# Routed tiles of a mixture-of-experts kernel: x transposed by DMA in 16-bit halves instead of by TensorE

## The chip, the cores and the metric

One Trainium2 chip; the kernel runs on one core of it. The metric is the device time of one execution in microseconds (us), lower is better. The engines are TensorE (PE in the profile; its weight loads are PEld), VectorE (DVE), ScalarE (ACT), GpSimd (POOL) and SyncE (SP), which only issues DMAs here.

## The reference

All numbers are float32. Two blocks run one after the other on 2048 tokens of width 256.

```python
x = x + xattn(layernorm(x), k, bias, ctx, ctx, 8)     # 256-tap causal convolutions of head products
x = x + ffn(layernorm(x))
# ffn, for all tokens xt (2048, 256):
scores = softmax(xt @ Wg.T)                           # 16 experts in 4 groups
# the best 2 groups by their maximum, in them the best 4 experts; weights = scores of these
h = silu(einsum('td,eid->eti', xt, W1)) * einsum('td,eid->eti', xt, W3)   # inner width 176
y = einsum('etd,te->td', einsum('eti,edi->etd', h, W2), combine)
z = silu(xt @ Ws1.T) * (xt @ Ws3.T) @ Ws2.T           # shared expert, inner width 352
return y + z
```

## The kernel before

The tokens are 16 units of 128. **First stage** (about 0 to 133 us): for each unit, ScalarE normalises, TensorE convolves with Toeplitz matrices (L1271, L1273), VectorE multiplies, and `norm2(u)` (L502) writes the unit's second layernorm into the first 256 columns of `rows[:, u, :]`. TensorE transposes these (`transpose_xn`) for the router and for the shared expert. A row of `rows` is 288 float32: 256 of x, then 16 gate weights and 16 destination numbers (together the "gates"). VectorE works the routing out in four batches of units; its exponentials are on ScalarE (L516). GpSimd scatters each row with four indirect DMAs (L661) to its four experts' regions of a DRAM buffer, `rows_scratch`.

**Second stage** (about 133 to 198 us): the shared expert (L1424, L1437), while VectorE ends the routing and writes the list of tiles.

**Third stage** (about 198 us to the end): 72 routed tiles of 128 rows of one expert, each engine with its own order of the steps. Tiles 16 to 23 are mixed: 64 rows of each of two experts. Of tile t:
- SP, `gather`: one plain DMA of 128 whole rows (144 KB) from `rows_scratch` into `xg[b]`, four buffers deep (L368); tiles 64 to 71 go to places in `rows` and are issued early (L410). Before each, SP loads the tile's start row from memory into a register and waits until tile t-4 has been transposed by TensorE and its gates taken by VectorE. Between the gathers SP issues other experts' weights, reads of results (L392) and stores.
- TensorE, in each step t: `up(t)` (L1382), `turn_x(t+1)` (L1403: two 128x128 transposes of the gathered rows into PSUM), `down(t-2)` (L1456), `turn_h(t-1)` (L1392).
- ScalarE, in each step: `silu(t)` (L553), `src_tr(t+1)` (L547: copies the transposed x from PSUM to `x_tr`), `store_y(t-2)` (L559).
- VectorE, in each step: `take(t)` (L1126: picks the expert's gate and destination), `hidden(t)` (L1089), `copy_h(t-1)` (L1096), `place(t)` (L1131: writes the destinations for the scatter, after the scatter of tile t-4 has landed). In steps 3 to 6 of each 8 from tile 32 on, one of four adds (L1200 to L1208) of results read back follows.
- GpSimd scatters each tile's y to `y_scratch` (L716).

Of the kernel before, what the change touches and what calls it, by code (L numbers as in the profile page):

```python
# [22 lines left out]
ACT = mybir.ActivationFunctionType  # L23
# [3 lines left out]
I32 = mybir.dt.int32  # L27
U32 = mybir.dt.uint32

P = 128  # L30
# [40 lines left out]
def build(nc, x_d, ctx_d, ctxt_d, ctxr_d, toep_d, bias_d, wg_d, experts_d, ws13_d, ws2_d, out_d):  # L71
    rows_d = nc.dram_tensor("rows_scratch", ((E + 1) * REGION, ROW), F32, kind="Internal").ap()
    y_d = nc.dram_tensor("y_scratch", (TOPK * TOK + 2 * E * P, L), F32, kind="Internal").ap()

    with ExitStack() as ctx:
# [26 lines left out]
        resid = sb("resid", [P, UNITS, L])  # L102
        rows = sb("rows", [P, UNITS, ROW])
# [6 lines left out]
        ident = sb("ident", [P, P])  # L110
        sum_i = sb("sum_i", [P, 2, 32])
        blocks = sb("blocks", [P, P])
# [37 lines left out]
        def carve(n):  # L150
# [47 lines left out]
        xt_ps = [bank[i][:, 0:L].rearrange("p (b n) -> p b n", b=LB) for i in (6, 7)]  # L198
# [15 lines left out]
        row_ready, xt_done, xnt_all = sem("row_ready"), sem("xt_done"), sem("xnt_all")  # L214
# [7 lines left out]
        rows_in = [sem(f"rows_in{b}") for b in range(DEPTH)]  # L222
        xtr_ps, xtr_ready, up_done, silu_done, hid_ready, ht_done, htr_ready, dn_done = (
            sem("xtr_ps"), sem("xtr_ready"), sem("up_done"), sem("silu_done"), sem("hid_ready"), sem("ht_done"),
# [8 lines left out]
        others_in = [sem(f"others_in{b}") for b in range(DEPTH)]  # L233
# [3 lines left out]
        block = ctx.enter_context(nc.Block())  # L237

# [36 lines left out]

        def rows_landed(eng, t, b, before):

            if is_late(t):
                eng.wait_ge(late_in[t - LIVE + LATE], 16)
            else:  # L280
                eng.wait_ge(rows_in[b], before * 16 + 16)

# [8 lines left out]
        def _(sp):  # L291
# [62 lines left out]

            def gather(t, b, before):
                if not (isinstance(t, int) and t < DEPTH):
                    sp.wait_ge(xtr_ps, t - (DEPTH - 1))
                    sp.wait_ge(taken, t - (DEPTH - 1))
                at = sp.value_load(tile_row[0:1, bass.ds(t, 1)], min_val=0, max_val=E * REGION)
# [3 lines left out]
                if is_mixed(t):  # L363
                    sp.dma_start(xg[b][0:HALF], rows_d[bass.ds(at, HALF)]).then_inc(rows_in[b], 16)
                    also = sp.value_load(other_row[0:1, t - MIXED0:t - MIXED0 + 1], min_val=0, max_val=E * REGION + HALF)
                    sp.dma_start(xg[b][HALF:P], rows_d[bass.ds(also, HALF)]).then_inc(others_in[b], 16)
                else:
                    sp.dma_start(xg[b], rows_d[bass.ds(at, P)]).then_inc(rows_in[b], 16)  # L368
# [96 lines left out]
        def _(act):  # L465
# [58 lines left out]
            for u in range(UNITS):  # L524
# [1039 lines left out]
```

## Time and profile before

| what | value |
|---|---|
| time, median of 3 runs | 398.21 us (396.35 to 399.11) |
| profiled execution, first to last instruction | 395.4 us (the profile gives no other time for it) |
| TensorE busy | 384.7 us, 97% |
| VectorE busy | 244.1 us, 62% |
| ScalarE busy | 162.9 us, 41% |
| GpSimd busy | 180.3 us, 46% |
| mean granted TensorE clock | 0.998 |

The page gives busy times of each engine, then groups of instructions by line with their count, busy time, mean and idle time before them. The trace behind it gives the same by stretch and in order of time.

### The profile page before, as it was taken

Reading aid. Unit: us, or ns where it says so; the run is one execution under the profiler, and the core shown is the slowest. Engines: PE = TensorE matmul, PEld = TensorE weight load, DVE = VectorE, ACT = ScalarE, POOL = GpSimd, SP = SyncE. Lnnn points to the kernel's source line nnn. Section 1 sums busy time; section 2 is a strip of 40 time slices with the busy share of each in tenths; the row PEclk is TensorE's granted clock in tenths of the full one; section 3 lists DMA queues with packets and bytes.
Section 4 is the critical chain, followed back from the end, with each engine's and each line's share of the span. In section 5 each row is a group of like instructions: output and inputs, shape, how many; then the busy total and the mean of one; then the engine's idle time right before and its main releaser. Section 6 shows DMA issues by size and latency. Waiting matters only on the chain.

```text
span 395.4 us, 9070 instructions
## 1 busy us (share of the span) xinstructions
PE 384.7 (97%) x2146; PEld 279.3 (71%) x2147; DVE 244.1 (62%) x676; ACT 162.9 (41%) x494; POOL 180.3 (46%) x225
## 2 busy tenths in 40 slices
PE   6999999999999999999999999999999999999996
PEld 6788888888888546555667675446767777777765
DVE  3577577987988465788735344443445464646466
ACT  5347656564564362101124333333333333334431
POOL 3254323337888573565553333333333333334333
PEclk9999999999999999999999999999999999999999
DMA  7974474368879996256376873334474737362737
GB/s 248 363 254 139 163 277 144 133 206 278 309 250 335 414 419 258 96 207 223 104 215 219 321 239 107 87 95 134 127 246 136 242 115 242 115 232 103 264 97 251
DMA packets 37812, 83.09 MB, mean 210 GB/s; under 512 B 5930, under 2 KB 25870, under 8 KB 35728
## 3 DMA queue, kind: packets, MB, share of 16 engines
q1 hardware_dynamic: 31248, 64.83, 49.1%
q0 software_dynamic: 6528, 17.84, 11.6%
q8 instruction: 16, 0.26, 0.3%
q14 instruction: 20, 0.16, 0.1%
HBM read 60.21 MB, written 23.48 MB: 212 GB/s over the span
## 4 chain that ended last, share of the span: by engine, by line
PE 79%; DVE 10%; DMA 4%; issue 2%; ACT 2%; SPq 1%; DVEq 1%; POOL 0%; POOLq 0%
PE heads L1382 18%; PE bank L1456 13%; PE heads L1271 11%; PE heads L1424 7%; PE heads L1273 5%; PE bank L1437 5%; PE heads L1392 4%; PE bank L1403 4%; PE bank L1285 3%; DVE kv L734 3%; PE heads L1374 3%; DMA toep<-toep_in 2%; PE bank L1448 2%; DVE prod L763 2%; DMA y_scratch<-toep,dest_i 2%
## 5 line engine op out<-in xcount | busy, mean ns | idle before, releaser
L716 POOL DMA_INDIRECT y_scratch<-toep,dest_i x72 | 71.8, 997 | 112.0 <-DVE dest_i L1131 96.0
L1382 PE MATMUL heads<-experts,toep 128*128 x256 | 86.6, 461 | 0.6 <-DVE toep L1089 0.5
L1271 PE MATMUL heads<-toep,kv 128*128 128x256 f32 x256 | 77.9, 386 | 1.9 <-DVE kv L734 0.8
L661 POOL DMA_INDIRECT rows_scratch<-rows,slot_i x64 | 63.3, 989 | 35.4 <-issue 19.5
L1456 PE MATMUL bank<-experts,toep 88*128 x256 | 66.2, 381 | 1.6 <-DVE toep L1096 1.6
L553 ACT ACTIVATE toep<-heads 128x176 f32<-128x176 f32 x72 | 22.8, 317 | 78.1 <-PE heads L1382 67.2
L1382 PEld LDWEIGHTS heads<-experts,toep 128*128 128x128 f32 x256 | 43.7, 190 | 14.8 <-issue 1.1
L1273 PEld LDWEIGHTS heads<-toep,kv 128*128 128x128 f32 x256 | 48.7, 190 | 6.5
L763 DVE TENSOR_TENSOR prod<-heads,ctx_rep 128x1024 f32<-128x1024 f32 x32 | 39.1, 1221 | 22.3 <-PE bank L1285 19.9
L1096 DVE COPY toep<-heads 88x256 f32<-88x256 f32 x72 | 30.2, 419 | 31.1 <-PE heads L1392 31.1
L1273 PE MATMUL heads<-toep,kv 128*128 128x128 f32 x256 | 49.2, 274 | 0.0
L1456 PEld LDWEIGHTS bank<-experts,toep 88*128 88x128 f32 x256 | 43.7, 190 | 6.1 <-issue 2.3
L559 ACT ACTIVATE toep<-bank 128x256 f32<-128x256 f32 x72 | 27.6, 383 | 39.5 <-PE bank L1456 34.1
L1424 PE MATMUL heads<-xn_tr_all,ws 128*128 128x512 f32 (+1 forms) x96 | 43.5, 596 | 0.0
L1089 DVE SCALAR_TENSOR_TENSOR toep<-toep,heads 128x176 f32<-128x176 f32 x72 | 28.6, 398 | 23.2 <-ACT toep L553 18.1
L1271 PEld LDWEIGHTS heads<-toep,kv 128*128 128x128 f32 x256 | 38.8, 192 | 2.6 <-issue 1.4
L734 DVE TENSOR_TENSOR kv<-bank,ctx_tr 128x2048 f32<-128x2048 f32 x15 | 34.2, 2282 | 0.1
L1403 PEld LDWEIGHTS bank<-ident,toep 128*128 128x128 f32 x128 | 17.3, 141 | 18.8 <-issue 12.4
L1424 PEld LDWEIGHTS heads<-xn_tr_all,ws 128*128 128x128 f32 (+1 forms) x96 | 16.9, 181 | 19.0 <-issue 18.4
L547 ACT ACTIVATE toep<-bank 128x256 f32<-128x256 f32 x72 | 27.5, 382 | 5.7 <-PE bank L1403 5.5
L1392 PE MATMUL heads<-ident,toep 128*88 128x128 f32 x144 | 27.8, 275 | 0.0
L1126 DVE COPY toep<-toep 128x2 f32 x56 | 10.1, 180 | 24.1 <-issue 15.1
(240 smaller groups left out, 513.4 us busy)
## 6 DMA issues: line engine op xcount, KB each, us to landing
ctx_rep<-ctxr_in SPq DMA_DIRECT2D x16, 1024.0 KB, 5.0
experts<-experts_in SPq DMA_DIRECT2D x16, 608.0 KB
toep<-rows_scratch SPq DMA_DIRECT2D x56, 144.0 KB
prod<-y_scratch SPq DMA_DIRECT2D x5, 1024.0 KB, 5.5
rows_scratch<-pad_row SPq DMA_DIRECT2D x17, 144.0 KB, 1.8
ctx_tr<-ctxt_in SPq DMA_DIRECT2D x16, 128.0 KB
toep<-toep_in SPq DMA_DIRECT2D x4, 512.0 KB, 7.0
ctx_n<-ctx_in SPq DMA_DIRECT2D x16, 128.0 KB, 2.1
```

What stands on the lines that cost most here:

```text
L661: pool.indirect_dma_start(rows_d, bass.IndirectOffsetOnAxis(ap=slot_i[:, u, k:k + 1].bitcast(U32), axis=0), rows[:, u, :], None).then_inc( ...
L716: pool.indirect_dma_start(y_d, bass.IndirectOffsetOnAxis(ap=dest_i[b][:, 0:1].bitcast(U32), axis=0), y_sb[b], None, bounds_check=TOPK * TO ...
L734: nc.vector.tensor_tensor(kv[:, u % 2, :, :].rearrange("p b (g i j) -> p (b g) i j", i=C, j=C), tr_ps.rearrange("p b (g i) -> p (b g) i", ...
L763: nc.vector.tensor_tensor(prod[:, par, :, :], y_ps[par], ctx_rep[:, u % 2, par::2, :], ALU.mult).then_inc(prod_ready, 1)
L1096: nc.vector.tensor_copy(hid_tr[p], ht_ps[p]).then_inc(htr_ready, 1)
L1271: nc.tensor.matmul(y_ps[par][:, i, :], kv[:, q, 0, h * P:(h + 1) * P], toep[:, q * HH + h, :], start=True, stop=False)
L1273: last = nc.tensor.matmul(y_ps[par][:, i, P:], kv[:, q, 1, h * P:(h + 1) * P], toep[:, q * HH + h, 0:P], start=False, stop=True)
L1382: last = nc.tensor.matmul(up_ps[p], x_tr[p][:, blk, :], up_w(e, blk), start=blk == 0, stop=blk == LB - 1)
L1392: last = nc.tensor.transpose(ht_ps[p][:, c, :], hid[p][:, c * HI:(c + 1) * HI], ident[:])
L1403: last = nc.tensor.transpose(xt_ps[p][:, blk, :], src[:, blk * P:(blk + 1) * P], ident[:])
L1424: last = nc.tensor.matmul(bank[2 * (s % 2) + w][0:rows_c, :].rearrange("p (u n) -> p u n", u=GT), ws13[:, blk, w, c0:c0 + rows_c], xn_tr_a ...
L1456: last = nc.tensor.matmul(dn_ps[p], hid_tr[p][:, c, :], down_w(e, c), start=c == 0, stop=c == 1)
```

## The change

x of a routed tile no longer passes TensorE and PSUM. ScalarE writes the layernorm of a unit into one buffer `xn` (TensorE transposes from there), and a new step `split_row` copies it, seen as 16-bit words, into `rows` with all low halves first and then all high halves. The scatter moves the same bytes, declared 16-bit. SP's gather becomes a DMA transpose of the 512 halves of 128 rows: it lands as four blocks of 128x128 halves, already transposed. VectorE puts low and high halves side by side again in `x_tr` (`weave`), for tile t+2 in step t, after `copy_h` and before `place`. `turn_x` and `src_tr` go. The gates come by a DMA of their own (128 bytes of each row) that ScalarE issues after `silu(w-2)` once the tile's x has landed; `take` waits for it. ScalarE's `store_y` of a tile stays at the same place of its order beside TensorE's. SP and ScalarE load four tiles' start rows at once into four registers.

```diff
+    halves_d = rows_d.bitcast(U16)
...
+        xn = sb("xn", [P, L])
...
+        def xn_of(u):
+            return spread[:] if u == UNITS - 1 else xn[:]
...
+        def in_halves(mem):
+            return mem[:, 0:L].bitcast(U16)
...
+            if is_mixed(t):
+                eng.wait_ge(others_in[b], (t - MIXED0) // DEPTH * 16 + 16)
+        def gates_landed(eng, t, b, before):
+            eng.wait_ge(gates_in[b], before * 16 + 16)
+            if is_mixed(t):
+                eng.wait_ge(other_gates[b], (t - MIXED0) // DEPTH * 16 + 16)
...
+            def turned(mem, at, lo, count):
+                return sp.dma_start_transpose(in_halves(mem).rearrange("p (r n) -> p r n", n=P)[:, :, lo:lo + count],
+                                              halves_d[bass.ds(at, count), 0:2 * L])
+            row_of, also_of, late_of = ([sp.alloc_register(f"{n}_of{b}") for b in range(DEPTH)] for n in ("row", "also", "late"))
             def gather(t, b, before):
+                if b == 0:
+                    sp.load(row_of, tile_row[0:1, bass.ds(t, DEPTH)])
+                    if is_mixed(t):
+                        sp.load(also_of, other_row[0:1, t - MIXED0:t - MIXED0 + DEPTH])
+                at = sp.snap(row_of[b], min_val=0, max_val=E * REGION)
                 if not (isinstance(t, int) and t < DEPTH):
-                    sp.wait_ge(xtr_ps, t - (DEPTH - 1))
-                    sp.wait_ge(taken, t - (DEPTH - 1))
-                at = sp.value_load(tile_row[0:1, bass.ds(t, 1)], min_val=0, max_val=E * REGION)
+                    sp.wait_ge(xtr_ready, t - (DEPTH - 1))
                 if isinstance(t, int) and t in (0, DEPTH):
                     need = sp.value_load(tile_need[0:1, t // DEPTH:t // DEPTH + 1], min_val=16 * TOPK * PACED, max_val=16 * TOPK * UNITS)
                     sp.wait_ge(scattered, need)
                 if is_mixed(t):
-                    sp.dma_start(xg[b][0:HALF], rows_d[bass.ds(at, HALF)]).then_inc(rows_in[b], 16)
-                    also = sp.value_load(other_row[0:1, t - MIXED0:t - MIXED0 + 1], min_val=0, max_val=E * REGION + HALF)
-                    sp.dma_start(xg[b][HALF:P], rows_d[bass.ds(also, HALF)]).then_inc(others_in[b], 16)
+                    turned(xg[b], at, 0, HALF).then_inc(rows_in[b], 16)
+                    also = sp.snap(also_of[b], min_val=0, max_val=E * REGION + HALF)
+                    turned(xg[b], also, HALF, HALF).then_inc(others_in[b], 16)
                 else:
-                    sp.dma_start(xg[b], rows_d[bass.ds(at, P)]).then_inc(rows_in[b], 16)
+                    turned(xg[b], at, 0, P).then_inc(rows_in[b], 16)
...
-                at = sp.value_load(tile_row[0:1, t:t + 1], min_val=0, max_val=E * REGION)
-                sp.dma_start(rows[:, UNITS - LATE + j, :], rows_d[bass.ds(at, P)]).then_inc(late_in[j], 16)
+                if j % DEPTH == 0:
+                    sp.load(late_of, tile_row[0:1, t:t + DEPTH])
+                at = sp.snap(late_of[j % DEPTH], min_val=0, max_val=E * REGION)
+                turned(rows[:, UNITS - LATE + j, :], at, 0, P).then_inc(late_in[j], 16)
...
                 act.wait_ge(b2, u + 1)
-                nc.scalar.activation(rows[:, u, 0:L], resid[:, u, :], ACT.Identity,
-                                     bias=ln2[:, u, 4:5], scale=ln2[:, u, 3:4]).then_inc(row_ready, 1)
+                if 1 <= u < UNITS - 1:
+                    act.wait_ge(xt_done, u)
+                nc.scalar.activation(xn_of(u), resid[:, u, :], ACT.Identity,
+                                     bias=ln2[:, u, 4:5], scale=ln2[:, u, 3:4]).then_inc(xn_ready, 1)
+            def split_row(u):
+                act.wait_ge(xn_ready, u + 1)
+                nc.scalar.activation(in_halves(rows[:, u, :]).rearrange("p (s l) -> p s l", s=2),
+                                     xn_of(u).bitcast(U16).rearrange("p (l s) -> p s l", s=2), ACT.Copy
+                                     ).then_inc(row_ready, 1)
...
+                if u >= 2:
+                    split_row(u - 2)
...
-            def src_tr(w, p):
-                if not (isinstance(w, int) and w < 2):
-                    act.wait_ge(up_done, w - 1)
-                act.wait_ge(xtr_ps, w + 1)
-                nc.scalar.activation(x_tr[p], xt_ps[p], ACT.Copy).then_inc(xtr_ready, 1)
+            gate_row, gate_also = ([act.alloc_register(f"{n}_of{b}") for b in range(DEPTH)] for n in ("gate_row", "gate_also"))
+            def load_gates(w, b, before):
+                rows_landed(act, w, b, before)
+                if b == 0:
+                    act.load(gate_row, tile_row[0:1, bass.ds(w, DEPTH)])
+                    if is_mixed(w):
+                        act.load(gate_also, other_row[0:1, w - MIXED0:w - MIXED0 + DEPTH])
+                at = act.snap(gate_row[b], min_val=0, max_val=E * REGION)
+                if not (isinstance(w, int) and w < DEPTH):
+                    act.wait_ge(taken, w - (DEPTH - 1))
+                gates = rows_of(w, b)[:, L:]
+                if is_mixed(w):
+                    act.dma_start(gates[0:HALF], rows_d[bass.ds(at, HALF), L:]).then_inc(gates_in[b], 16)
+                    also = act.snap(gate_also[b], min_val=0, max_val=E * REGION + HALF)
+                    act.dma_start(gates[HALF:P], rows_d[bass.ds(also, HALF), L:]).then_inc(other_gates[b], 16)
+                else:
+                    act.dma_start(gates, rows_d[bass.ds(at, P), L:]).then_inc(gates_in[b], 16)
...
             copy_xn(UNITS - 1)
+            split_row(UNITS - 2)
             silu_shared(2)
+            split_row(UNITS - 1)
             copy_logits(UNITS - 1)
...
-            def routed_step(t, b, before):
+            def routed_step(w, b, before):
                 p = b % 2
-                silu(t, p)
-                if not (isinstance(t, int) and t == LIVE - 1):
-                    src_tr(t + 1, 1 - p)
-                if not (isinstance(t, int) and t < 2):
-                    store_y(t - 2, p, (b - 2) % DEPTH, before if b >= 2 else before - 1)
-            routed(act, routed_step, 2 * DEPTH)
-            for t in range(LIVE - 2, LIVE):
+                if not (isinstance(w, int) and w < 2):
+                    silu(w - 2, p)
+                load_gates(w, b, before)
+                if not (isinstance(w, int) and w < 4):
+                    store_y(w - 4, p, b, before - 1)
+            routed(act, routed_step, MIXED0 + MIXED + DEPTH)
+            for t in range(LIVE - 4, LIVE):
+                if t < LIVE - 2:
+                    silu(t + 2, t % 2)
...
-                        rows_d, bass.IndirectOffsetOnAxis(ap=slot_i[:, u, k:k + 1].bitcast(U32), axis=0),
-                        rows[:, u, :], None).then_inc(scattered, 16)
+                        halves_d, bass.IndirectOffsetOnAxis(ap=slot_i[:, u, k:k + 1].bitcast(U32), axis=0),
+                        rows[:, u, :].bitcast(U16), None).then_inc(scattered, 16)
...
+            def weave(w, b, before):
+                if not (isinstance(w, int) and w < 2):
+                    dve.wait_ge(up_done, w - 1)
+                rows_landed(dve, w, b, before)
+                nc.vector.tensor_copy(x_tr[b % 2].rearrange("p b n -> p (b n)").bitcast(U16).rearrange("p (n s) -> p n s", s=2),
+                                      in_halves(rows_of(w, b)).rearrange("p (s n) -> p n s", s=2)).then_inc(xtr_ready, 1)
...
-                rows_landed(dve, t, b, before)
+                gates_landed(dve, t, b, before)
...
+                if not (isinstance(t, int) and t >= LIVE - 2):
+                    weave(t + 2, (b + 2) % DEPTH, before + 1 if b >= 2 else before)
...
+            for w in range(2):
+                weave(w, w, 0)
             for m in range(4):
                 steps(m, 0, 8)
-            with dve.Fori(4, 8) as m:
+            with dve.Fori(4, 7) as m:
                 steps(m, 0, 8, m - 4, m * 2 - 8)
+            steps(7, 0, 8, 3, 6)
...
-                pe.wait_ge(row_ready, u + 1)
+                pe.wait_ge(xn_ready, u + 1)
                 if u >= 1:
                     pe.wait_ge(xnt_all, u)
                     pe.wait_ge(logits_ready, u)
                 for blk in range(LB):
-                    last = nc.tensor.transpose(xn_ps[:, blk, :], rows[:, u, blk * P:(blk + 1) * P], ident[:])
+                    last = nc.tensor.transpose(xn_ps[:, blk, :], xn_of(u)[:, blk * P:(blk + 1) * P], ident[:])
...
-            def turn_x(t, p, b, before):
-                src = rows_of(t, b)
-                rows_landed(pe, t, b, before)
-                if is_mixed(t):
-                    pe.wait_ge(others_in[b], (t - MIXED0) // DEPTH * 16 + 16)
-                if not (isinstance(t, int) and t < 2):
-                    pe.wait_ge(xtr_ready, t - 1)
-                for blk in range(LB):
-                    last = nc.tensor.transpose(xt_ps[p][:, blk, :], src[:, blk * P:(blk + 1) * P], ident[:])
-                last.then_inc(xtr_ps, 1)
...
-            turn_x(0, 0, 0, 0)
...
                 up(t, p, b)
-                if not (isinstance(t, int) and t == LIVE - 1):
-                    turn_x(t + 1, 1 - p, (b + 1) % DEPTH, before + 1 if b == DEPTH - 1 else before)
```

## Rows read from the trace of the kernel before

**Rows 1.** The page, busy time and share of the span by engine.
```profile
PE 384.7 (97%) x2146; PEld 279.3 (71%) x2147; DVE 244.1 (62%) x676; ACT 162.9 (41%) x494; POOL 180.3 (46%) x225
```
**Rows 2.** Windows: start:end, span, busy by engine (instructions), PE clock, DMA share, GB/s.
```profile
305.00:325.00 20.00, 20.00 (x98) 14.82 (x97) 10.82 (x36) 7.86 (x24) 7.95 (x9) 1.00 0.54 177
```
**Rows 3.** TensorE in order of time, one tile: start, duration, line, tiles, count.
```profile
300.27 1.35 PE L1382 MATMUL heads<-experts,toep 128*128 x4
301.45 0.38 PE L1403 MATMUL bank<-ident,toep 128*128 128x128 f32 x2
301.67 1.03 PE L1456 MATMUL bank<-experts,toep 88*128 x4
302.54 0.39 PE L1392 MATMUL heads<-ident,toep 128*88 128x128 f32 x2
302.76 1.35 PE L1382 MATMUL heads<-experts,toep 128*128 x4
```
**Rows 4.** TensorE's lines L1403 and L1382 alone: durations min/median/max ns, first and last start.
```profile
L1403 PE MATMUL bank<-ident,toep x128: 271/273/329, 197.1 to 361.3; 128*128 128x128 f32 x128
L1403 PE MATMUL bank<-ident,rows x16: 272/273/273, 363.7 to 381.2; 128*128 128x128 f32 x16
...
L1382 PE MATMUL heads<-experts,toep x256: 457/460/558, 198.6 to 383.3; 128*128 x128
```
**Rows 5.** VectorE in order of time; in brackets the idle time before and its releaser.
```profile
293.70 0.15 DVE L1131 CAST dest_i<-toep 128x1 int32<-128x1 f32 x1 [0.78 <-DMA y_scratch<-toep,dest_i]
294.59 0.17 DVE L1126 COPY toep<-toep 128x2 f32 x1 [0.74 <-DVE dest_i L1131]
294.90 0.40 DVE L1089 SCALAR_TENSOR_TENSOR toep<-toep,heads 128x176 f32<-128x176 f32 x1
295.21 0.41 DVE L1096 COPY toep<-heads 88x256 f32<-88x256 f32 x1
295.55 0.14 DVE L1131 CAST dest_i<-toep 128x1 int32<-128x1 f32 x1
295.61 0.68 DVE L1200 TENSOR_TENSOR prod<-prod 128x512 f32<-128x512 f32 x1
296.29 0.17 DVE L1126 COPY toep<-toep 128x2 f32 x1
...
302.96 0.42 DVE L1096 COPY toep<-heads 88x256 f32<-88x256 f32 x1 [0.56 <-PE heads L1392]
```
**Rows 6.** Waits from 230 to 390 us: total us, times, longest.
```profile
DVE dest_i L1131 <- DMA y_scratch<-toep,dest_i: 2.4, 5, 0.8
```
**Rows 7.** Groups by line, ScalarE: busy us, mean ns, idle before.
```profile
L502 ACT ACTIVATE rows<-resid,ln 128x256 f32<-128x256 f32 x16 | 9.6, 600 | 0.5
```
**Rows 8.** DMA view: the queue of SP, and issues with KB each and us to landing.
```profile
q1 hardware_dynamic: 31248, 64.83, 49.1%
...
toep<-rows_scratch SPq DMA_DIRECT2D x56, 144.0 KB
...
y_scratch<-toep,dest_i POOLq DMA_INDIRECT x72, 2.9
...
rows<-rows_scratch SPq DMA_DIRECT2D x8, 144.0 KB, 2.5
```
**Rows 9.** SP's queue in order of time.
```profile
292.46 0.33 SPq L410 DMA_DIRECT2D rows<-rows_scratch  x1
293.68 0.33 SPq L368 DMA_DIRECT2D toep<-rows_scratch  x1
```
**Rows 10.** Start of the third stage, SP's queue and VectorE.
```profile
194.35 8.09 SPq L368 DMA_DIRECT2D toep<-rows_scratch  x6
```
```profile
197.28 0.42 DVE L1110 TENSOR_TENSOR resid<-bank,resid 128x256 f32<-128x256 f32 x1 [0.80 <-PE bank L1437]
```
**Rows 11.** First stage, ScalarE and VectorE in order of time.
```profile
96.63 0.29 ACT L490 ACTIVATE ln<-ln 128x1 f32<-128x1 f32 x1 [0.64 <-POOL ln L637]
```
```profile
96.02 0.22 DVE L826 TENSOR_REDUCE route_tmp<-route_tmp 128x4 f32<-128x64 f32 x1 [1.51 <-ACT route_tmp L516]
97.04 1.23 DVE L763 TENSOR_TENSOR prod<-heads,ctx_rep 128x1024 f32<-128x1024 f32 x1 [0.32 <-PE bank L1285]
```

More of the change, by code:

```diff
@@ L27 @@
 I32 = mybir.dt.int32
+U16 = mybir.dt.uint16
 U32 = mybir.dt.uint32
@@ L110, in build @@
         ident = sb("ident", [P, P])
+        blocks = xn[:, 0:P]
         sum_i = sb("sum_i", [P, 2, 32])
-        blocks = sb("blocks", [P, P])
         skip_w = sb("skip_w", [P, 2, P])
@@ L197, in build @@
         dn_ps = [bank[i][:, 0:L] for i in (4, 5)]
-        xt_ps = [bank[i][:, 0:L].rearrange("p (b n) -> p b n", b=LB) for i in (6, 7)]
         wait_taken = sem("wait_taken")
@@ L213, in build @@
         m2, q2, e2, p2, b2 = sem("mean2"), sem("square2"), sem("vareps2"), sem("rstd2"), sem("shift2")
-        row_ready, xt_done, xnt_all = sem("row_ready"), sem("xt_done"), sem("xnt_all")
+        xn_ready, row_ready, xt_done, xnt_all = sem("xn_ready"), sem("row_ready"), sem("xt_done"), sem("xnt_all")
         logits_done, logits_ready = sem("logits_done"), sem("logits_ready")
@@ L221, in build @@
         s_up, s_silu, s_hid, s_down = sem("shared_up"), sem("shared_silu"), sem("shared_hid"), sem("shared_down")
-        rows_in = [sem(f"rows_in{b}") for b in range(DEPTH)]
-        xtr_ps, xtr_ready, up_done, silu_done, hid_ready, ht_done, htr_ready, dn_done = (
-            sem("xtr_ps"), sem("xtr_ready"), sem("up_done"), sem("silu_done"), sem("hid_ready"), sem("ht_done"),
+        rows_in, gates_in = ([sem(f"{n}_in{b}") for b in range(DEPTH)] for n in ("rows", "gates"))
+        xtr_ready, up_done, silu_done, hid_ready, ht_done, htr_ready, dn_done = (
+            sem("xtr_ready"), sem("up_done"), sem("silu_done"), sem("hid_ready"), sem("ht_done"),
             sem("htr_ready"), sem("dn_done"))
@@ L232, in build @@
         other_in = [sem(f"other_in{g}") for g in range(MIXED)]
-        others_in = [sem(f"others_in{b}") for b in range(DEPTH)]
+        others_in, other_gates = ([sem(f"{n}{b}") for b in range(DEPTH)] for n in ("others_in", "other_gates"))
         added, finished = sem("added"), sem("finished")
@@ L587, in _ @@
                 silu_shared(s)
-            src_tr(0, 0)
-            def routed_step(t, b, before):
+            def routed_step(w, b, before):
                 p = b % 2
-                silu(t, p)
-                if not (isinstance(t, int) and t == LIVE - 1):
-                    src_tr(t + 1, 1 - p)
-                if not (isinstance(t, int) and t < 2):
-                    store_y(t - 2, p, (b - 2) % DEPTH, before if b >= 2 else before - 1)
-            routed(act, routed_step, 2 * DEPTH)
-            for t in range(LIVE - 2, LIVE):
+                if not (isinstance(w, int) and w < 2):
[7 more added lines that the diff above has]
+                    silu(t + 2, t % 2)
                 store_y(t, t % 2, t % DEPTH, t // DEPTH)
@@ L1120, in take @@
                 if is_mixed(t):
-                    dve.wait_ge(others_in[b], (t - MIXED0) // DEPTH * 16 + 16)
                     nc.vector.tensor_copy(picked[0:HALF, b, :].unsqueeze(2), gates[0:HALF, :, bass.ds(e, 1)])
@@ L1516, in _ @@
                 down(t, t % 2, t % DEPTH)
-            pe.wait_ge(xtr_ready, LIVE)
             for i in range(2):
```

## The prediction

> **What bounds the kernel now.** I read the busy times first: TensorE 97%, no other engine above 62% [rows 1]. A share is a mean over stages, so next the windows of the third stage: in 305 to 325 us TensorE is busy for all 20.00 us, VectorE for 10.82 and ScalarE for 7.86, at full clock [rows 2]. Then TensorE in order of time. One step runs from `up` at 300.27 to the next `up` at 302.76, 2.49 us, and splits by starts into `up` 1.18, `turn_x` 0.22 (301.45 to 301.67), `down` 0.87 and `turn_h` 0.22 [rows 3]. A matmul's duration overlaps its neighbour's, so the difference of starts is what an instruction costs here, not its 0.27 us in the group of L1403. TensorE itself is the limit, and what leaves its queue is time saved as long as nothing else takes 2.27 us or more in a step.
>
> **What goes.** L1403 has 128 + 16 records, two for a tile: 72 tiles, from 197.1 to 381.2 us [rows 4]. 72 x 0.22 = 15.8 us off TensorE. That is the whole prize. `src_tr` leaves ScalarE, which waits for TensorE anyway: nothing.
>
> **Does TensorE run on without the transposes?** `turn_h` now ends at about 302.9 (302.54 + 0.39), its copy runs 302.96 to 303.38, and the `down` that reads it starts 1.18 + 0.22 after the `up` at 302.76, so at 304.16 [rows 3, 5]. Spare 0.78 us, 0.56 after the change. `hidden(t-1)` lies a whole step ahead of `turn_h(t-1)`. So TensorE finds its operands, if VectorE doesn't fall behind by more than 0.56.
>
> **VectorE.** The trace has no copy of 16-bit words. Bounds: the add of 128x512 takes 0.68 us for as many elements as `weave` has (512); the copy of 128x256 float32 takes 0.42 for as many bytes [rows 5]. I take 0.62, near the upper end, since `weave` reads low and high halves by turns from two places. The dense stretch 294.59 to 296.29 gives the costs by starts: `take` 0.31, `hidden` 0.31, `copy_h` 0.34, `place` 0.06, add 0.68, with `take` following at once [rows 5]. Without an add a step is 1.02 + 0.62 = 1.64, and up to 0.33 more when the load of the expert's number isn't hidden (my estimate from starts; the gap ahead of `take` at 294.59 is 0.74 with a wait in it): 1.97, under 2.27. With an add it is 1.64 + 0.68 = 2.32, 0.05 over; four such steps in a row make 0.2, inside the 0.56 of spare. Cost 0.5 us over the 20 steps with adds; 0 with a `weave` of 0.42, 2 with 0.68 plus waits.
>
> The Trainium skill (VectorE: DVE Perf Modes, What auto-detection actually checks) lets a one-source copy in SBUF take two elements a cycle by using both ports; and (SBUF — State Buffer, on the shared port pair) such a copy shuts GpSimd out for its duration. No row shows either yet; `weave` would then be near the lower bound and each scatter up to that much later, a delay that falls into the term of the next paragraph.
>
> **`place` and the scatter of y.** `place(t)` waits until the scatter of tile t-4 has landed, and `take`, `hidden` and everything else of VectorE queue behind it. This wait is not quite covered now: VectorE stood 0.78 us for it at 293.70, just after a read-back of 1 MB was started, and 5 times from 230 to 390 us, 2.4 us in all [rows 5, 6]. A scatter lands 2.9 us after its issue [rows 8]; with steps 0.22 shorter, the two steps or so between a scatter and the reuse of its buffer lose 0.44 us. In the six or so stretches with a read-back that is about 0.4 each, 2.5 us; I take 2, between 0 and 5.
>
> **SP and the DMA engines.** Before, SP held 0.33 us for each gather, 1.2 us from one to the next with the register load between [rows 9]. After, one load serves four gathers. `gather(t)` now waits for `weave(t-4)`, which runs in step t-6, and its x is read in step t-2: four steps, 9 us, for what took 2.5 us as a plain copy [rows 8]. So latency is hidden; throughput isn't. The trace shows no DMA transpose. Lower bound, the same bytes at the mean rate of SP's queue: 64.83 MB in 49.1% of 395.4 us is 334 GB/s, 128 KB take 0.4 us [rows 8]. Upper bound: this queue's packets took 0.491 x 395.4 x 16 / 31248 = 99 ns each; should each of a tile's 128 x 4 pieces of 256 bytes cost a full packet, 512 x 99 / 16 = 3.2 us a tile [rows 8]. I take 0.4 to 1.5 us, nearer the lower, since the same queue moves the same rows: cost nothing, because it stays below 2.27.
>
> Two pages of the Trainium skill disagree here. Advanced Engine Details and Errata (X-Bar Transpose) holds transposing DMAs to be as fast as plain ones; VectorE: DVE Perf Modes (The three transpose paths) lists 1309 ns for one 128x128 block of 16-bit elements. An estimate from the latter is 4 x 1.31 = 5.2 us a tile, which, if blocks don't overlap, would put the kernel near 398 + 72 x 2.7 = 594 us.
>
> **ScalarE.** `load_gates` is an issue of some 0.33 us [rows 9] in place of a copy; it waits for x two steps ahead, and the gates have about two steps, 4.5 us, to land, against 2.5 for the larger copy: nothing. In the first stage `split_row` adds 16 operations. L502 takes 0.60 us for 256 elements with a bias and scale [rows 7]; I take 0.6. ScalarE idles 0.64 ahead of the next unit's shift [rows 11], which covers it in 13 units. In the three units with exponentials it delays them by 0.6, and VectorE, which waits for them 1.51 us, has 0.32 of spare ahead of the next product [rows 11]: 3 x 0.3 = 0.9. I take 1.0 with the end of the stage; between 0 and 3.
>
> **The start of the third stage.** The first gather is issued at 194.35 [rows 10], and x would be there at 196.9. VectorE's last add of the shared expert ends at 197.7 [rows 10], then two weaves: x of tile 0 at 198.3, where the first `up` started at 198.6 [rows 4]. Covered if the transpose lands within 3.3 us; each microsecond over that costs one. The gates of tile 0 come about 2.8 us after its x, at 199.7, and the first `hidden` follows as soon as `silu` does. I take 0.5, between 0 and 3.
>
> **Sum.** -15.8 + 0.5 + 2 + 1 + 0.5 = -11.8 us. The profiled execution spans 395.4, so it would span 383.6. The median of the runs is 398.2, 2.8 above that span, and I keep the 2.8: 386.4. With the bounds, -15.8 gives 382.4 and +13 of costs gives 395.4. Its own range is 382 to 393.
>
> **Rivals.**
> 1. Transposes bound the third stage. Place: the DMA engines, or SP's queue if it is held while the blocks are issued; then `weave` and `load_gates` wait for x and TensorE waits for `x_tr`. It decides at 2.27 us a tile for the loss of any gain, and at 2.49 for a loss. At the upper bound of 3.2: 398.2 + 72 x (3.2 - 2.49) = 449 us. For it: blocks of 256-byte pieces, and on SP everything else (read-backs, stores) queues behind. Against: nothing in the trace is that slow for these bytes. Chance 0.20. The page with 1309 ns a block belongs to this case.
> 2. The gain is given back on VectorE: `weave` at 0.68 with its start gap, `place` waiting at every read-back, and the load exposed, so a step is 2.4 in half of the steps. 72 x (2.49 - 2.4) = 6.5, less the 1.5 of the other stages: 5 us, 393. For it: VectorE goes from 54% [rows 2] to over 85%. Against: the spare of 0.56. Chance 0.14.
> 3. TensorE's step doesn't shrink, because what follows the transposes takes their time (the weight load of `down`, or `turn_h` waiting). Rows 3 show no gap around L1403 that the next instruction could fall into; 398. Chance 0.04.
>
> **How the numbers follow.** My forecast has 0.62. Of it nearly all is faster by over 1% (below 394.2); a measurement of this kernel can't tell less than about 1%. Rival 2 lies half there and half within 1%. Rival 1 is slower but for a small part near its point of decision. Faster 0.68, same 0.13, slower 0.19. The range takes in the forecast's own, rivals 2 and 3 and the first part of rival 1: 381 to 405.
>
> **What would show it.** Right: steps of 2.27 us between `up`s, L1403 gone, no idle TensorE beyond 1 us outside read-backs, `weave` at 0.4 to 0.7, x landing within 4 us of its issue. Wrong: SP's issues one after another without waits, idle TensorE released by `weave`, x landing many microseconds after issue (rival 1); VectorE without gaps, its waits for the scatter grown (rival 2). What I know least is the price of a DMA transpose, on SP and on the DMA engines alike.

## The result and the profile after

| | before | after |
|---|---|---|
| time, median | 397.67 us (396.35 to 399.11, 4 runs) | 402.34 us (400.34 to 403.89, 4 runs) |
| ratio | | 1.011, 95% interval 1.0081 to 1.0139 |
| profiled execution | span 395.4 us | span 402.1 us |
| mean granted TensorE clock | 0.998 | 0.983 |

The forecast was 386.4 us, faster. The kernel became about 1% slower; 402.34 lies within the range of 381 to 405, on the side of rival 1. The profiled execution is of the slowest of the four runs, 403.89 us; the granted clock of the other three was 0.991 to 0.996. Its stalls are those of a run slower than the median.

The page, busy time and share by engine, with ScalarE's, VectorE's and the DMA groups that matter (the counterpart of [rows 1] and [rows 8]):

```profile
PE 379.1 (94%) x2002; PEld 269.1 (67%) x2003; DVE 267.2 (66%) x748; ACT 147.7 (37%) x439; POOL 185.4 (46%) x225
...
q1 hardware_dynamic: 60176, 63.65, 51.6%
...
L1154 DVE COPY toep<-toep 128x512 uint16<-128x512 uint16 x64 | 27.0, 421 | 7.3 <-DMA toep<-rows_scratch 7.2
```

TensorE lost 144 instructions, its transposes of x, but only 5.6 us of busy time, in part because some of what is left ran at a lower clock. `weave` (L1154) takes 0.42 us. SP's queue moves about the same bytes as before in twice the packets, 60176 for 31248.

TensorE in order of time, where nothing disturbs it (the counterpart of [rows 3]):

```profile
276.57 1.35 PE L1451 MATMUL heads<-experts,toep 128*128 x4
277.76 1.03 PE L1514 MATMUL bank<-experts,toep 88*128 x4
278.62 0.38 PE L1461 MATMUL heads<-ident,toep 128*88 128x128 f32 x2
278.84 1.35 PE L1451 MATMUL heads<-experts,toep 128*128 x4
```

A step is 278.84 - 276.57 = 2.27 us. The saving exists, at its predicted size. The line of `up` alone gives the whole stage:

```profile
L1451 PE MATMUL heads<-experts,toep x256: 457/459/950, 198.9 to 390.0; 128*128 x128
```

From the first `up` to the last it is 191.1 us; before, it was 383.3 - 198.6 = 184.7 [rows 4]. The first `up` starts 0.3 us later than before, so the first two stages cost next to nothing and all of the loss is in the third. Sixteen of its 71 intervals from one tile's `up` to the next are above 2.7 us and together 24.0 us over 2.27 each: 10.8 of it ahead of tiles 5 to 14, while the other experts are loaded, and 5.7 ahead of tiles 44 and 45. The longest (5.64 us, from 312.57 to 318.21), in the order in which the engines wait: SP's queue, VectorE and TensorE.

```profile
300.28 7.94 SPq L375 DMA_TRANSPOSE toep<-rows_scratch  x4
309.21 0.42 SPq L423 DMA_DIRECT2D out<-resid  x1
309.99 0.40 SPq L420 DMA_DIRECT2D prod<-y_scratch  x1
311.48 7.92 SPq L375 DMA_TRANSPOSE toep<-rows_scratch  x5
```

```profile
312.77 0.42 DVE L1161 COPY toep<-heads 88x256 f32<-88x256 f32 x1 [0.26 <-PE heads L1461]
317.64 0.43 DVE L1154 COPY toep<-toep 128x512 uint16<-128x512 uint16 x1 [4.44 <-DMA toep<-rows_scratch]
```

```profile
312.57 1.35 PE L1451 MATMUL heads<-experts,toep 128*128 x4
...
314.62 0.38 PE L1461 MATMUL heads<-ident,toep 128*88 128x128 f32 x2
318.21 2.71 PE L1451 MATMUL heads<-experts,toep 128*128 x4 [3.21 <-DVE toep L1154]
320.72 1.91 PE L1514 MATMUL bank<-experts,toep 88*128 x4
322.42 0.64 PE L1461 MATMUL heads<-ident,toep 128*88 128x128 f32 x2
322.85 1.85 PE L1451 MATMUL heads<-experts,toep 128*128 x4
```

x of tile 44 is issued at 311.48, behind a store and a read-back of 1 MB, and VectorE has it at 317.64: 4.44 us of waiting in `weave`, then 3.21 in `up`. So SP issued it only 1.7 us before VectorE was ready for it (313.19, the end of `copy_h`), and it took 6.2 us to arrive, beside the read-back. The DMA engines were full meanwhile (a share of 1.02 in 311 to 318 us, the last number but one):

```profile
311.00:318.00 7.00, 4.01 (x19) 2.77 (x17) 1.74 (x7) 0.32 (x1) 0.98 (x1) 0.93 1.02 260
```

The same `up` then takes 2.71 us in place of 1.35, and TensorE's granted clock in 318 to 323 us is half:

```profile
318.00:323.00 5.00, 4.79 (x11) 3.23 (x12) 2.55 (x10) 1.63 (x5) 1.97 (x2) 0.50 0.47 106
```

That is its lower level, 1.2 GHz for 2.4, just after TensorE stood idle for 3.21 us. The next interval (318.21 to 322.85) is 4.64 us, with no wait in it.

The price of a transpose, from its line alone (duration ns min/median/max, then the time to landing); [rows 9] had 0.33 us of SP for a plain copy, and [rows 8] 2.5 us to landing:

```profile
L375 SPq DMA_TRANSPOSE toep<-rows_scratch x72: 1170/1202/2069, 194.6 to 357.0; - x72
...
DMA to landing us min/median/max: 2.6/3.7/4.5
```

And the waits of the third stage (195 us to the end; total us, times, longest us):

```profile
ACT toep L612 <- DVE toep L1190: 12.7, 5, 6.6
ACT toep L612 <- DMA toep<-rows_scratch: 9.0, 4, 2.9
DVE dest_i L1195 <- DMA y_scratch<-toep,dest_i: 8.0, 12, 1.4
DVE toep L1154 <- DMA toep<-rows_scratch: 7.2, 4, 4.4
DVE toep L1190 <- DMA toep<-rows_scratch: 4.7, 3, 2.2
```

The third was there before as well. Over the same stretch of the kernel before it is

```profile
DVE dest_i L1131 <- DMA y_scratch<-toep,dest_i: 6.0, 9, 1.5
```

([rows 6] has 2.4 us for 230 to 390 us; there it is 6.7 after the change.) In these rows L612 is `store_y`, which stands behind `load_gates`; L1195 is `place`, L1154 `weave`, and L1190 `take`, waiting for its gates. So there are three suspects: x late (SP's queue or the DMA engines), gates late, and the wait in `place`.

### The profile page after: what moved, and what is told of

It is laid out like the page before. It is cut to its first block, busy times and chain, and to the rows that moved or that the text cites. A ratio compares the mean times of both kernels' runs of the same rounds, so it can differ in the third digit from the quotient of the medians.

```text
span 402.1 us, 8727 instructions
## 1 busy us (share of the span) xinstructions
PE 379.1 (94%) x2002; PEld 269.1 (67%) x2003; DVE 267.2 (66%) x748; ACT 147.7 (37%) x439; POOL 185.4 (46%) x225
## 3 DMA queue, kind: packets, MB, share of 16 engines
q1 hardware_dynamic: 60176, 63.65, 51.6%
## 4 chain that ended last, share of the span: by engine, by line
PE 39%; DMA 17%; issue 13%; DVE 10%; SPq 9%; POOL 8%; ACT 2%; DVEq 1%; ACTq 0%; POOLq 0%
PE heads L1340 9%; DMA toep<-rows_scratch 7%; POOL rows_scratch L718 7%; PE heads L1451 7%; PE bank L1514 6%; SPq L375 5%; PE heads L1342 4%; DMA y_scratch<-toep,dest_i 3%; DVE kv L791 3%; PE bank L1354 3%; PE heads L1443 3%; DMA toep<-toep_in 2%; PE heads L1461 2%; DMA rows_scratch<-rows,slot_i 2%; DVE prod L820 2%
## 5 line engine op out<-in xcount | busy, mean ns | idle before, releaser
L773 POOL DMA_INDIRECT y_scratch<-toep,dest_i x72 | 76.6, 1064 | 111.4 <-DVE dest_i L1195 62.6
L1451 PE MATMUL heads<-experts,toep 128*128 x256 | 91.2, 480 | 4.4 <-DVE toep L1154 4.0
L1514 PE MATMUL bank<-experts,toep 88*128 x256 | 69.2, 394 | 10.6 <-DVE toep L1161 10.6
L1514 PEld LDWEIGHTS bank<-experts,toep 88*128 88x128 f32 x256 | 48.0, 193 | 34.5 <-issue 22.5
L1451 PEld LDWEIGHTS heads<-experts,toep 128*128 128x128 f32 x256 | 45.5, 197 | 21.6 <-issue 8.5
L612 ACT ACTIVATE toep<-bank 128x256 f32<-128x256 f32 x72 | 27.7, 384 | 84.0 <-PE bank L1514 43.6
L1154 DVE COPY toep<-toep 128x512 uint16<-128x512 uint16 x64 | 27.0, 421 | 7.3 <-DMA toep<-rows_scratch 7.2
L1190 DVE COPY toep<-toep 128x2 f32 x56 | 10.0, 179 | 24.9 <-issue 14.8
L1461 PEld LDWEIGHTS heads<-ident,toep 128*88 128x88 f32 x144 | 17.3, 125 | 11.2 <-issue 2.8
```

Source lines behind the costliest of these rows:

```text
L773: pool.indirect_dma_start(y_d, bass.IndirectOffsetOnAxis(ap=dest_i[b][:, 0:1].bitcast(U32), axis=0), y_sb[b], None, bounds_check=TOPK * TO ...
L1451: last = nc.tensor.matmul(up_ps[p], x_tr[p][:, blk, :], up_w(e, blk), start=blk == 0, stop=blk == LB - 1)
L1461: last = nc.tensor.transpose(ht_ps[p][:, c, :], hid[p][:, c * HI:(c + 1) * HI], ident[:])
L1514: last = nc.tensor.matmul(dn_ps[p], hid_tr[p][:, c, :], down_w(e, c), start=c == 0, stop=c == 1)
```

## The experiments

Ratios are to the kernel before on the same chip, with 95% intervals. The runs stand on several chips, so a difference between two of them is read from medians only where the intervals of the ratios are apart. "Plain" kernels move x without transposing it, so their x is in the wrong order and their output isn't the reference's; all sizes and waits are those of the real one. A round is eight tiles of the third stage; a late gather is the early issued one of a tile from 64 to 71; a read-back reads 1 MB of results for VectorE's adds.

**1. Transposes or plain copies (e1, e2, e7).**

```diff
-  sp.dma_start_transpose(in_halves(mem).rearrange(...)[:, :, lo:lo + count], halves_d[bass.ds(at, count), 0:2 * L])
+  sp.dma_start(in_halves(mem)[lo:lo + count], halves_d[bass.ds(at, count), 0:2 * L])            # e1
+  sp.value_load(tile_e[0:1, 0:1], ...)      # e2: once ahead of each gather; e7: twice
```

> The changed kernel with each DMA transpose replaced by a plain DMA of the same 1 KB of the same rows, so x reaches the routed tiles untransposed; all else stays, the 16-bit weave too. Theory A (SP's queue is what is short: a transpose holds it 1.20 us where a plain issue holds it 0.34, and x comes late after each burst of SP's other work): 384 to 389 us, gathers far ahead again, stalls of up at tiles 7 to 12 and 44 to 46 mostly gone. Theory B (the cause is the new order: x and gates are wanted two tiles earlier, in the middle of VectorE's and ScalarE's queues, whoever moves them): 396 to 402 us, stalls at the same tiles. Theory C (it is the transposes' time on the DMA engines): also near 386, to be told from A by the next run.

> The same plain copies, but SP loads one more value from memory ahead of each gather, 0.7 to 0.8 us, so that its queue is held about as long as by a transpose (0.34 + 0.75 against 1.20). Theory A: back up to 396 to 402 us with the stalls after tile 7 and after each read-back. Theory C: stays within 2 us of the plain run, since the DMA engines have the plain copies' load.

> Plain copies of x (untransposed), with two loaded values ahead of each gather: SP's queue is held for 0.34 + 1.5 us a gather, more than a transpose holds it. The first held run came to no more than the plain one, but its hold was 0.1 to 0.3 us short of a transpose's with what follows it. Theory A as refined (SP falls behind when its work per tile passes 2.27 us, with the late gathers and the loads of the other experts): 398 to 404 us. If the hold doesn't matter: 392 to 396.

Measured: e1 394.65 us, 0.9894 (0.9865 to 0.9923); e2 393.95, 0.9897 (0.9863 to 0.9932); e7 411.17, 1.0331 (1.0268 to 1.0394). The transposes cost 7.7 us (402.34 to 394.65), but without them 8 us are still missing from the forecast; e1 fell between the times of its theories. SP's wait for `weave` says how far SP runs ahead of the tiles. It is, with the transposes and in e1 (each from its own list of waits):

```profile
SPq L375 <- DVE toep L1154: 6.6, 11, 1.6
```

```profile
SPq L375 <- DVE toep L1153: 57.3, 42, 2.9
```

SP's slack of 57.3 us shrinks to 6.6. In e7 a gather together with a late gather takes SP 3.5 us, more than a step, and of such waits 0.2 us are left: there SP bounds the stage. In e2 it keeps 18.3 us of slack and nothing is lost. So a longer hold of the queue cost nothing while slack was left (e2), and 16.5 us once it was gone (e7).

**2. Relief for the burst (e3, e4, e8).** Each moves one thing out of the way of x with the transposes kept.

```diff
 def round_of(m):                                   # e3
-    ... store; read_back; gathers(m, DEPTH, 2 * DEPTH)
+    ... gathers(m, DEPTH, DEPTH + 2); store; read_back; gathers(m, DEPTH + 2, 2 * DEPTH)
 def routed_step(w, b, before):                     # e4
-    load_gates(w, b, before); store_y(...)
+    store_y(...); load_gates(w, b, before)
-    others' expert loads issued by SP             # e8
+    the same loads issued by ScalarE behind load_gates and ahead of store_y
```

> The changed kernel with transposes; in each round of 8 tiles the gathers of its fifth and sixth tile are issued ahead of the store and the read-back of 1 MB, not behind them. Theory A and the reading that x of tile 8m+4 lands behind the read-back in the same rings: the stalls at tiles 36, 44, 52, 60 and 68 (13 us in all) shrink by half or more, 394 to 398 us. If the stalls come from the DMA engines being full in that stretch, whoever is first: 401 to 404.

> The changed kernel with ScalarE's store_y of tile w-4 ahead of load_gates(w) in its queue. If ScalarE waiting in load_gates for a late x (9.0 us of its waits by landings, 12.7 by the take behind it) is what holds back y, the scatter and so place, 398 to 401 us; if late x stalls VectorE's weave anyway, no change, 401 to 404.

> The changed kernel with the loads of the mixed tiles' other experts (eight of 608 KB) issued by ScalarE, at the same tiles. SP then has only transposes from tile 8 to 15, 1.3 us each, and they queue behind no such load. If SP's queue is what is late there: the stalls at tiles 9 to 14 (10 us) shrink to under 5, 396 to 399 us. If the DMA engines are full with the loads: 401 to 404.

Measured: e3 403.68, 1.0101 (1.0055 to 1.0146), the stall moved from tile 44 to 38, 39 and 46 (7.71 us); e4 402.20, 1.0115 (1.0053 to 1.0177); e8 405.75, 1.0143 (1.0104 to 1.0181), with 7.88 us at tile 12. No order of the same work helped. In e8 SP's slack rose to 18.8 us and the time did not fall, but its loads then stood in ScalarE's queue ahead of `store_y`, so it doesn't clear SP.

**3. `place` and `take` (e5, e6, e9).** e5 doubles the destination buffers, so that `place(t)` waits for the scatter of t-8. e6 is e5 with plain copies. e9 loads the gates one step earlier and takes ScalarE's wait for x away: two edits in one.

```diff
-  dest_i = [... for i in range(DEPTH)]             # e5, e6
+  dest_i = [... for i in range(2 * DEPTH)]
-      at_least(dve, y_sent[b], before * 16)
+      at_least(dve, y_sent[b], (before - 1) * 16)
-  load_gates(w, b, before)                         # e9, from step 8 on
+  load_gates(w + 1, (b + 1) % DEPTH, ...)          # and no rows_landed(act, ...) in it
```

> The changed kernel with eight buffers of destinations in place of four, so that VectorE's place(t) waits for the scatter of tile t-8 and never stands. Theory D (what the plain run still lost, about 10 us, is place waiting for a scatter of y that lands late beside a read-back, with take and hidden behind it): 394 to 398 us. If late x stalls weave in the same stretches anyway: 400 to 403.

> Plain copies of x (untransposed, as before) and eight buffers of destinations. Theory D: 384 to 388 us, steps of 2.27 us nearly throughout, no stall at tiles 35, 44, 52, 60. If the rest is something else (the gates, ScalarE's queue, the DMA engines): 391 to 394.

> The changed kernel; from tile 9 on ScalarE issues the gates' load of tile w+1 where it issued that of tile w, and no longer waits for x of that tile first. Theory E (beside a read-back or the other experts' loads a small load takes 5 us and more; the gates are issued two steps, some 4.2 us, ahead of take, which then stands with hidden and copy_h behind it; ScalarE's own wait for x delays store_y): alone 397 to 400 us, since place and the late x are left. If place and late x fall into the same places and hide it: 401 to 404.

Measured: e5 403.04, 1.0096 (1.0061 to 1.0131): nothing. e6 391.77, 0.9871 (0.9806 to 0.9936): 2.9 us under e1 by the medians, but the intervals overlap, so it isn't clear of noise. e9 398.30, 1.0007 (0.9977 to 1.0036): 4.0 us under the changed kernel. In e6 the wait of `place`, 10.8 us in e1, is gone, and much of it turned up in `take`, which with four places waited 5.1 us in e1:

```profile
DVE toep L1189 <- DMA toep<-rows_scratch: 11.5, 6, 3.0
```

**4. Both waits mended (e10, e11, e12).** e10 is plain with both edits, e11 has the transposes with both, and e12 spreads the other experts' loads and the late gathers over more tiles.

> Plain copies of x (untransposed), eight buffers of destinations and the early gates. Theories D and E together: the whole loss of the plain run is in place and take, so 383 to 387 us, with a stall over 0.5 us at three tiles or fewer after tile 12. If there is a third cause that isn't the transposes': 388 to 392.

> As the run before but with the transposes. What it is above that one is the price of transposing by DMA with nothing else late: by theory C, x lands too late only beside the bursts, 3 to 8 us more, so 388 to 394 us. If the transposes cost the full 9 us that the first plain run showed whatever else is mended: 392 to 396.

> As the run before, with the other experts' loads one for every two tiles (tiles 5 to 19 instead of 5 to 14) and the early gathers of the last tiles one for every two gathers (from tile 24) instead of four of them in a row right behind the first read-back. If the bursts on SP's queue and the DMA engines make x late, 4 to 6 us under the run before: 383 to 388 us, ahead of both kernels. If x is late whatever the bursts: no change to the run before.

Measured: e10 385.57, 0.9693 (0.9671 to 0.9716); e11 394.23, 0.9905 (0.9877 to 0.9932); e12 394.67, 0.9933 (0.9899 to 0.9967). So the two edits for the waits of VectorE are worth 9.1 us with plain copies (394.65 to 385.57) and 8.1 with transposes (402.34 to 394.23), and the transposes 8.7 us (385.57 to 394.23). e12 was no faster than e11: the stall ahead of tile 44 went and one of 4.95 us ahead of tile 36 came. The window in which the first other experts are loaded shows what the DMA engines do meanwhile (the last two numbers are their busy share and GB/s), for e10 and then e11:

```profile
198.00:228.00 30.00, 27.43 (x114) 18.66 (x113) 18.42 (x71) 6.94 (x20) 14.18 (x15) 1.00 0.82 277
```

```profile
198.00:228.00 30.00, 25.55 (x99) 17.14 (x99) 16.08 (x64) 5.86 (x17) 13.11 (x14) 0.94 0.94 241
```

With transposes the engines are busier (0.94 for 0.82) and move less (241 for 277 GB/s): a transpose takes more of their time for its bytes than a plain copy. Over the whole span it is little: SP's queue has 51.6% of 402.1 us as changed and 48.0% of 393.0 in e1, 207.5 and 188.6 us, and the difference over 72 tiles is 0.26 us a tile.

**5. What the 8.7 us are made of (g1, g3, g4, g5, g6).** All start from e10, but g1 from e11. g3 holds SP by a register load. g4 writes a row in four pieces of 256 bytes. g5 has both, and g6 is g4 again over more rounds. g1 takes SP's four loads of send counts out of each round.

```diff
+  sp.value_load(tile_e[0:1, 0:1], ...)                                              # g3 (g5: for three of four)
-  sp.dma_start(in_halves(mem)[lo:lo + count], halves_d[...])                        # g4, g5, g6
+  sp.dma_start(in_halves(mem)[...].rearrange("p (r n) -> p r n", n=P)[:, ::-1, :], halves_d[...].rearrange(...))
-  for b in range(DEPTH): gathers(m, b, b + 1); sends.append(sends_of(m - 4, b))     # g1
+  gathers(m, 0, DEPTH); sends = [m * 32 - 32] * DEPTH
```

> Plain copies with both waits mended (x is not transposed), and one more register load ahead of each, so that SP is held about as long for a tile as by a transpose. If the transposes' 8.7 us are SP's time: 392 to 395, with the stalls at the same tiles as with the transposes. If they are landing time or load on the DMA engines: 385.6 within 1 us, with SP still ahead.

> Plain copies with both waits mended (x is not transposed), but each row is written in four pieces of 256 bytes in reverse order, so that the DMA engines handle as many and as small packets as for a transpose while SP is held 0.33 us. VectorE reads the halves in the other order to match. If the packets' size is what the transposes cost: 392 to 395, with x landing at 3.6 us in place of 2.6. If it is SP's time: 385.6 within 1 us.

> The transposes with both waits mended, and SP relieved of the loads of send counts: the read-backs of rounds wait on constants in their place, so each round of eight tiles has four loads fewer on SP. If SP's occupied queue is what makes x late after a burst, SP gets some 4 us more in a round: the stalls at tiles 20, 21, 44 and 45 shrink, and the time goes from 394.2 towards 390. If landing is what makes x late, it stays at 394, within 1 us.

> Plain copies with both waits mended (x is not transposed), written in pieces of 256 bytes and with one more register load ahead of three of four, so that both costs of a transpose are there together: SP held about 1.4 us for a tile, and its packets on the DMA engines. Each alone left the kernel at 386 (held) and 389 (pieces). If a transpose's 8.7 us come from the two together, this is at 392 to 395; if something else in a transpose costs the time, at 386 to 389.

> The pieces of 256 bytes alone, once more and over more rounds, since the first look had times from 382.6 to 389.5. If packets alone cost something, its median is at 388 to 389 again; if not, at 386 within 1 us.

Measured: g3 386.06, 0.9698 (0.9652 to 0.9744); g4 388.81 (382.56 to 389.47; too wide for a ratio); g6, the same kernel on another chip, 385.91, 0.9704 (0.9676 to 0.9732), so two medians of one kernel can lie 2.9 us apart; g5 390.79, 0.981 (0.976 to 0.986); g1 390.01, 0.9782 (0.9717 to 0.9847). By the ratios each alone (g3, g6) is within 1 us of nothing, and the two together are 5.2 us by the medians (385.57 to 390.79) and 4.7 by the ratios. With them the stall at tile 44 and 45 is back (5.25 and 4.03 us). SP's slack, for e10, g6, g3, g5 and e11 in this order:

```profile
SPq L375 <- DVE toep L1159: 50.1, 43, 2.0
```

```profile
SPq L375 <- DVE toep L1160: 33.1, 34, 1.8
```

```profile
SPq L375 <- DVE toep L1161: 13.2, 20, 1.7
```

```profile
SPq L375 <- DVE toep L1164: 9.1, 11, 1.4
```

```profile
SPq L375 <- DVE toep L1160: 1.7, 5, 0.5
```

Time and slack go together: 385.6, 385.9, 386.1, 390.8, 394.2 us. How the slack decides is seen at tile 44. Its x is issued before the `up` of tile 42 starts by 2.9 us in e10 and in g6, 1.9 in g3 and 2.7 in g1, and there `weave` doesn't wait for it and the step is 2.3 us; in g5 it is issued 0.0, in the changed kernel 1.2 and in e11 1.4 us after that start, `weave` waits 4.1 to 4.4 us, and the interval is 5.3 to 5.6. In these three x arrived 7.0, 6.2 and 5.9 us after its issue, beside the read-back, and the 7.0 are of plain pieces. The lead doesn't decide alone: in g4, the kernel of g6 once more, x took 7.4 us and `weave` waited 1.6 with 2.9 us of lead.

g1 is the test of this from the other side: four register loads fewer in a round, the same DMAs, and the time falls by 4.2 us, with a slack of 5.3. (Its read-back waits for constants, not for loaded counts; it is not later for that, at 302.24 us for 307.80 in e11.) Its steps in 300 to 320 us have no idle TensorE, where e11 had 16.74 us busy of 20:

```profile
300.00:320.00 20.00, 20.00 (x89) 14.47 (x87) 14.61 (x49) 5.93 (x17) 9.31 (x9) 1.00 0.77 197
```

```profile
300.00:320.00 20.00, 16.74 (x66) 11.58 (x65) 10.42 (x36) 4.53 (x14) 7.09 (x7) 0.91 0.68 180
```

(g1 first.) g1 is the fastest that computes the reference: 2.2% under the kernel before and 3.1% under the change as made. The eight destination buffers were not tried on the kernel before, whose `place` waited too, so how much of the 2.2% they would give there alone is open. The stand-ins are a little short: the pieces of g5 and g6 land in 3.0 and 3.2 us in the median against 3.6 for e11's transposes, and where late gathers alternate, a gather to the next is 1.1 us in g3 and 1.3 in g5 in the mean, against 1.35 for transposes. So g3 shows that a hold of 1.1 us is free, not that 1.35 is, and the 3.4 us between g5 and e11 can be this rest, the longer landing or the DMA engines' load; they were not separated.

## Why the prediction was wrong

- **TensorE's saving**: right. The step is 2.27 us, and e10 ran at it.
- **`weave`**: better than taken, 0.42 for 0.62 us, at the lower bound. 512 elements take the 0.42 us that [rows 5] has for a copy of half as many. The two elements a cycle of the Trainium skill (VectorE: DVE Perf Modes, What auto-detection actually checks) agree with that. Whether such a copy holds GpSimd up was not tested; its scatters of y are 1064 ns in the mean after 997. VectorE stayed at 66%, so rival 2's dense VectorE did not arise; the other half of it, a longer wait in `place`, did, from 2.4 to 6.7 us in 230 to 390 us (6.0 to 8.0 in the whole stage).
- **ScalarE in the first stage and the start**: 1 and 0.5 us taken, 0.3 measured for both together.
- **The gates' load: the first step that failed.** I had "about two steps, 4.5 us, to land, against 2.5 for the larger copy: nothing". 2.5 us was the median over the late gathers of the kernel before; the slowest of them, issued at 289.6 us just behind a read-back, took 4.4. `take` waits up to 3.0 us for its gates in e6, and `load_gates` itself starts late, since it waits for x and, in ScalarE's queue, for `silu`. Moving it a step ahead and taking its wait for x away gave 4.0 us (e9); which of the two did it was not separated.
- **`place`**: 2 us taken, between 0 and 5. Its mending alone gave nothing that is clear of noise (e5, e6), since the wait then moves to `take`. Together the two gave 8 to 9 us where the sum had 2, so 6 to 7 are missing here. The bounds were made for each wait by itself, and both stand in one in-order queue: the price has to be put on the queue.
- **SP and the DMA engines: the second step that failed**, by 8.7 us. "Cost nothing, because it stays below 2.27" compared a transpose alone with a step. SP holds 1.20 us for it, 0.87 more than the 0.33 of [rows 9], and a step's other issues come on top. In the changed kernel's queue, one tile is a transpose, a load of another expert and register loads:

```profile
214.13 0.36 SPq L405 DMA_DIRECT2D xn_tr_all<-experts_in  x1
215.03 1.22 SPq L375 DMA_TRANSPOSE toep<-rows_scratch  x1
217.08 0.34 SPq L405 DMA_DIRECT2D xn_tr_all<-experts_in  x1
217.61 1.21 SPq L375 DMA_TRANSPOSE toep<-rows_scratch  x1
```

  From 215.03 to 217.61 are 2.58 us, above 2.27. In such stretches SP falls behind, and elsewhere it gains at most 2.27 - 1.35 = 0.9 us a tile (1.35 is from one transpose to the next, with the register work). "Four steps, 9 us" were there only for an SP with slack. The right comparison was all of SP's work in a round of eight tiles with 8 x 2.27 = 18.2 us, and its point of decision is that sum, not a single transpose. For tiles 40 to 47 SP needed 17.8 us as changed (from 300.28 on, with no wait until 318.1), 15.0 in the kernel before and 10.2 in e10; for 32 to 39, with the late gathers, 21.5, 17.0 and 11.0. For the mixed tiles 16 to 23 it was 24.1, 20.5 and 12.6: each takes two transposes of 64 rows, and such a half-sized one holds SP as long (1.17 us at least) as one of 128. The load on the DMA engines was small in the mean, as I had it (0.26 us a tile more), but in 311 to 318 us, where x was late, they were full.
- **The two pages of the Trainium skill.** The 1309 ns a block (VectorE: DVE Perf Modes, The three transpose paths) did not turn into 5.2 us a tile: a tile's four blocks hold SP for 1.20 us and land in 3.7. Nor were the transposes as fast as plain copies, as Advanced Engine Details and Errata of the Trainium skill (X-Bar Transpose) has it: 3.7 us for 2.6 in e1, and a fuller DMA with fewer GB/s.
- **Rival 1** was the right direction with the right place, SP's queue, but not its form. It was to set in when a transpose takes 2.27 us on each tile, and cost 50 us. It sets in at the bursts and costs some 8 us (7.7 from e1, 8.7 from e10). What makes it decide the sign is the other loss: plain copies as changed (e1) are 1.1% faster than before, with transposes 1.1% slower. That 402.34 lies in the range is in part luck: its upper end came from rival 1 alone, and about half of the distance to the forecast comes from VectorE's two waits.
- **The clock**: not in the sum. An idle TensorE of 3.21 us is followed by an `up` at half clock and an interval of 4.64 us, so a stall at tile 44 of 3.4 us (5.64 - 2.27) costs 5.7 (with 4.64 - 2.27 for the next). The mean granted clock of the profiled executions is 0.983 as changed, 0.991 in e11 and 0.994 in g1.

The sum again with what was measured: -15.8 (transposes) + 9 (VectorE's two waits) + 8.7 (DMA transposes, with the clock) + 0.3 gives +2.2 us; the medians differ by 4.7. The rest of 2.5 is not assigned to a cause, but 1.7 of it can be seen: from the last `up` to the end its profiled run takes 13.8 us, where the kernel before and the changed one take 12.1.

## What to carry to other kernels

Cost a slower issue against the queue's whole work over a round, not against one step: the queue's wait for a free buffer, summed, is the slack that it may use up, and two costs that were free alone were 5 us together here, when both drew on it. Give a small load that is newly split off a lead of its own; a median landing time is no bound for it beside a burst. When several waits stand in one in-order engine, price the queue: here, mending one of them moved much of its time to the next.

## What the hardware showed unexpectedly

- A DMA transpose of 128 rows by 512 16-bit elements holds SP's queue 1.20 us in the median (1.17 to 2.07 over 72, the 16 of only 64 rows among them), where a plain DMA of the same rows takes 0.33, and one written in four pieces a row 0.62.
- Its packets are of 256 bytes (SP's queue has 60176 packets for 31248), and it lands in 3.7 us. In 198 to 228 us the engines were busy 0.94 for 241 GB/s with it (e11), and 0.89 for 269 with plain pieces of that size (g6).
- A 16-bit copy of 128x512 elements with every second element picked takes 0.42 us on VectorE, SBUF to SBUF.
- TensorE's granted clock was 0.50 in the 5 us after an idle time of 3.21 us, and 0.93 in the 7 us that hold it.
